# A two-layer deformable convolution in f32: the dense interpolation matmuls of layer 2 cut from 64x128 of the array and 384 columns to 64x64 and 352 columns

## What is computed

```python
x = x + L0(gn(x))    # 4 sampled positions a pixel, softmax weights, 1x1 projection, batch norm, gelu
x = x + L1(gn(x))    # 3x3 deformable convolution
```

```python
p = offset + p_0 + p_n                       # tap position, fractional
x_off = g_lt*gather(lt) + g_rb*gather(rb) + g_lb*gather(lb) + g_rt*gather(rt)
x_off = x_off * m                            # the gate
out = conv2d(x_off, w_conv, stride=3)        # sum over taps and channels
```

## Time and profile before

| | |
|---|---|
| median of three runs | 597.45 us |
| the profiled execution, its own time | 598.6 us |
| its span | 596.8 us |
| PE busy | 492.7 us (83%) |
| DVE busy | 453.8 us (76%) |
| GpSimd (POOL) busy | 379.1 us (64%) |
| ACT busy | 233.7 us (39%) |
| L1408, DVE multiply by the row hats | 144 instructions, some 950 ns each |
| L1416, DVE addition of row halves | 64 instructions, 955 ns |
| L993, PE dense interpolation | 640 records for 320 matmuls |

### The profile page before, as it was taken

The page is one execution under the profiler, slowest core; times in us unless marked ns, Lnnn a source line. Parts: engine busy times, 40 slices in busy tenths (PEclk is TensorE's granted clock), DMA queues, the critical chain, the costliest instruction groups (busy, mean ns, idle before and its releaser), DMA issues.

```text
span 596.8 us, 10350 instructions
## 1 busy us (share of the span) xinstructions
PE 492.7 (83%) x3568; PEld 296.3 (50%) x3568; DVE 453.8 (76%) x935; ACT 233.7 (39%) x407; POOL 379.1 (64%) x350
## 2 busy tenths in 40 slices
PE   0393699987740655989999999999999999999996
PEld 0271477665420422445555565555655555555554
DVE  2926489999648755576978878988898898898781
ACT  0543113321249557653434344334433433433311
POOL 5048167778725473564777777777777777777740
PEclk9975579999895756889999999999999999999999
DMA  9651746857400491121222222921221122122110
GB/s 196 170 182 36 167 101 142 175 125 165 107 24 0 150 115 28 35 58 32 74 78 72 72 71 72 120 54 49 56 56 53 51 54 58 49 54 55 52 39 11
DMA packets 44114, 48.58 MB, mean 81 GB/s; under 512 B 24858, under 2 KB 34458, under 8 KB 43556
## 3 DMA queue, kind: packets, MB, share of 16 engines
q1 hardware_dynamic: 33172, 25.67, 19.3%
q0 software_dynamic: 10752, 22.04, 14.6%
q10 hardware_dynamic: 144, 0.24, 0.2%
HBM read 39.01 MB, written 8.91 MB: 80 GB/s over the span
## 4 chain that ended last, share of the span: by engine, by line
PE 65%; DVE 10%; issue 7%; ACT 7%; POOL 5%; DMA 4%; SPq 1%; DVEq 0%; POOLq 0%; ACTq 0%
PE ps_later L993 9%; PE ps_pair L993 9%; PE ps_raw L977 8%; PE ps_x L1005 7%; PE ps_raw L836 6%; PE ps_o L1035 5%; PE ps_x L1014 4%; PE ps_x L1008 3%; PE ps_pair L816 3%; PE ps_o L849 3%; POOL got L496 3%; ACT xn L570 2%; PE ps_later L873 2%; PE ps_x L895 2%; DVE vlast L1408 2%
## 5 line engine op out<-in xcount | busy, mean ns | idle before, releaser
L496 POOL DMA_INDIRECT got<-table,idx x336 | 355.5, 1058 | 179.4 <-issue 123.0
L1408 DVE TENSOR_TENSOR vprod<-ps_pair,rhat 128x768 f32<-128x768 f32 x64 | 60.9, 952 | 7.5 <-PE ps_pair L993 7.4
L1599 DVE TENSOR_TENSOR prod<-got,wgt 128x512 f32<-128x512 f32 x84 | 57.4, 683 | 9.5 <-DMA got<-table,idx 9.3
L1408 DVE TENSOR_TENSOR vprod<-ps_later,rhat 128x768 f32<-128x768 f32 x64 | 60.6, 947 | 3.3 <-PE ps_later L993 3.2
L1416 DVE TENSOR_TENSOR vprod<-vprod 128x768 f32<-128x768 f32 x64 | 61.1, 955 | 1.2
L977 PE MATMUL ps_raw<-conv_out,later 128*128 128x512 f32 x96 | 58.7, 696 | 2.2 <-ACT shared L717 1.4
L1005 PEld LDWEIGHTS ps_x<-early,vprod 128*128 128x128 f32 x384 | 43.3, 144 | 33.0 <-issue 23.5
L1005 PE MATMUL ps_x<-early,vprod 128*128 128x128 f32 x384 | 55.1, 280 | 0.7 <-DVE vlast L1419 0.5
L1591 DVE TENSOR_TENSOR samples<-shared,vprod 128x800 f32<-128x800 f32 x44 | 42.9, 983 | 10.9 <-DMA shared<-positions 7.7
L816 PE MATMUL ps_pair<-early,xn 128*128 128x128 f32 (+1 forms) x136 | 21.0, 313 | 34.5 <-POOL xn L487 24.1
L704 ACT ACTIVATE samples<-ps_x 128x384 f32<-128x384 f32 x64 | 27.9, 488 | 53.9 <-PE ps_x L1014 53.5
(11 more groups left out here) (171 smaller groups left out, 813.5 us busy)
## 6 DMA issues: line engine op xcount, KB each, us to landing
shared<-positions SPq DMA_DIRECT2D x22, 440.0 KB, 6.3
table<-trow SPq DMA_DIRECT2D x24, 256.0 KB, 2.1
got<-table,idx POOLq DMA_INDIRECT x336
raw<-in_x SPq DMA_DIRECT2D x16, 256.0 KB, 10.0
y<-table SPq DMA_DIRECT2D x4, 512.0 KB, 8.2
out<-ysumT SPq DMA_DIRECT2D x64, 16.0 KB
later<-in_later SPq DMA_DIRECT2D x1, 514.5 KB
positions<-prow SPq DMA_DIRECT2D x2, 256.0 KB, 2.3
```

Of the source, the lines that this page charges most:

```text
L496: pool.indirect_dma_start(into[t][:, s * P:(s + 1) * P], None, tab, bass.IndirectOffsetOnAxis(ap=idx[:, slot, k:k + 1], axis=0),).then_inc ...
L1408: nc.vector.tensor_tensor(dst, ps_dense[pair_number(0, t, pair) % 2][:].rearrange("p (d n) -> p d n", d=2)[:, :, 0:WROWS * C].rearrange("p ...
L1599: nc.vector.tensor_tensor(into[:, t % 2, 0:S * P].rearrange("p (n c) -> p n c", c=C), came[:, t, 0:S * P].rearrange("p (n c) -> p n c", c= ...
```

## The change

A tile's two image rows get eleven rows of `xcol` each, instead of twelve together. A pair is four matmuls: for each image row `r` of the tile and each tap `h`, the weights are 64 x 64 of `chat` (the 64 pixels of that image row), the moving operand is 11 x 32 = 352 columns of `xcol` that begin one row lower for `r` = 1, and the result goes to partitions 64 `r` to 64 `r` + 63 of the tap's bank. `v_mm` counts four per pair. The row hats are built for 11 steps, and the table `grid1` loses the shift of one row for the second half of the partitions. DVE multiplies 2 x 11 x 32 = 704 elements. Of eleven rows, rows 6 to 10 are added to rows 0 to 4 and row 5 stays as it is, so PE still turns six rows.

```diff
-WROWS = 2 * REACH1 + 2
-XROWS = H - 1 + WROWS
+WROWS = 2 * REACH1 + 1
+XROWS = H + WROWS
+HALF = (WROWS + 1) // 2
...
-                    pe.wait_ge(v_mm, 2 * PAIRS * (g - 1))
+                    pe.wait_ge(v_mm, 4 * PAIRS * (g - 1))
...
-                for h in range(2):
-                    at, tap = (t + h, 8) if pair == 2 else (t, GT + 2 * pair + h)
-                    top = (g % GB) * GROWS + 2 * at + tap // 3 - 1
-                    nc.tensor.matmul(ps_dense[n % 2][:, h * GPIX:h * GPIX + WROWS * C],
-                                     chat[g % 2][W * h:W * (h + 1), pair, at * P:(at + 1) * P],
-                                     xcol[b][W * h:W * (h + 1), top * C:(top + WROWS) * C],
-                                     start=True, stop=True).then_inc(v_mm, 1)
+                for r in range(2):
+                    for h in range(2):
+                        at, tap = (t + h, 8) if pair == 2 else (t, GT + 2 * pair + h)
+                        top = (g % GB) * GROWS + 2 * at + tap // 3 - 1 + r
+                        nc.tensor.matmul(ps_dense[n % 2][W * r:W * (r + 1), h * GPIX:h * GPIX + WROWS * C],
+                                         chat[g % 2][W * h:W * (h + 1), pair, at * P + W * r:at * P + W * (r + 1)],
+                                         xcol[b][W * h:W * (h + 1), top * C:(top + WROWS) * C],
+                                         start=True, stop=True).then_inc(v_mm, 1)
...
-                for r in range(WROWS // 2):
+                for r in range(HALF):
...
-                    dve.wait_ge(v_mm, 2 * n + 2)
+                    dve.wait_ge(v_mm, 4 * n + 4)
...
-                half = WROWS // 2
+                half = WROWS - HALF
                 nc.vector.tensor_tensor(vprod[:, t % 2, 0:half, :], vprod[:, t % 2, 0:half, :],
-                                        vprod[:, t % 2, half:WROWS, :], ALU.add).then_inc(v_added, 1)
+                                        vprod[:, t % 2, HALF:WROWS, :], ALU.add).then_inc(v_added, 1)
...
-    grid1[:, GT:9] = REACH1 + (p // W)[:, None]
+    grid1[:, GT:9] = REACH1
```

More of the change, by code:

```diff
@@ L1003, in turn_samples @@
                     pe.wait_ge(trans_copied, n)
-                for r in range(WROWS // 2):
+                for r in range(HALF):
                     nc.tensor.matmul(ps_x[1][:, P:2 * P], vprod[:, t % 2, r, :], idn[:], start=(r == 0),
-                                     stop=(r == WROWS // 2 - 1), is_transpose=True)
-                for r in range(0, WROWS // 2, 2):
+                                     stop=(r == HALF - 1), is_transpose=True)
+                for r in range(0, HALF, 2):
                     last = nc.tensor.matmul(ps_x[1][0:2 * C, 2 * P:3 * P],
                                             vlast[:, t % 2, r:r + 2, :].rearrange("p w c -> p (w c)"), idn[:],
-                                            start=(r == 0), stop=(r + 2 == WROWS // 2), is_transpose=True)
+                                            start=(r == 0), stop=(r + 2 == HALF), is_transpose=True)
                 last.then_inc(v_turned, 1)
@@ L1414, in weigh_rows @@
                 dve.wait_ge(v_read, pairs_done(g, t))
-                half = WROWS // 2
+                half = WROWS - HALF
                 nc.vector.tensor_tensor(vprod[:, t % 2, 0:half, :], vprod[:, t % 2, 0:half, :],
-                                        vprod[:, t % 2, half:WROWS, :], ALU.add).then_inc(v_added, 1)
+                                        vprod[:, t % 2, HALF:WROWS, :], ALU.add).then_inc(v_added, 1)
                 if t % 2 == 0:
                     nc.vector.tensor_tensor(vlast[:, :, 0:half, :], vlast[:, :, 0:half, :],
-                                            vlast[:, :, half:WROWS, :], ALU.add).then_inc(v_added, 1)
+                                            vlast[:, :, HALF:WROWS, :], ALU.add).then_inc(v_added, 1)
             def next_gather_places(i, k, made):
```

## The result

| | before | after |
|---|---|---|
| median | 598.1 us (597.41 to 600.13, four runs) | 589.31 us (588.95 to 589.44) |
| profiled execution, its span | 598.6, 596.8 us | 589.18, 587.4 us |
| PE busy | 492.7 us | 480.7 us |
| DVE busy | 453.8 us | 431.5 us |
| one group, from group 7 on | 21.34 us | 20.42 us |

The ratio is 0.985 (95% 0.981 to 0.988), 8.8 us less. The forecast was 584.0, in a range of 581 to 590. One further execution of the changed kernel took 1141.93 us and is left out as disturbed.

The account below looks back on a forecast made before the run. PE was taken to bound the kernel, with DVE setting the pace for 0.23 us a group. PE's 12.6 and the waits' 1.0 gave 13.6 us off 598.6; the median forecast was 584.0 us, range 581 to 590.

Parts of the forecast that it names:

- rival 2: GpSimd sets the end: DVE's work adds 0.04 us to each of the last 144 gathers, 588 us; chance 0.15.
- What a pair is made of: PE's pair alone, 0.84 us before: 0.107 exposed weight load, 0.64 for two passes, about 0.095 wait before another shape.
- four matmuls of 64 x 64: PE's new pair: the four run together, load 0.053; 0.098 us less for a pair alone, 0.146 for a run of two.
- Rival 1: On PE, the four matmuls go two by two: a pair costs 1.38 us instead of 0.84, 678 us; chance 0.10.
- PE's part: Shorter pairs on PE in layer 2's groups, summed over groups 0 to 15: 12.6 us gained.
- DVE's waits: Two places in a group where PE waits for DVE; their shrinking gains 1.0 us, ends 0 and 1.6.
- DVE's operations: DVE's shorter L1408, L1416 and L1419: 885, 822 and 484 ns, worth nothing by themselves beside PE.
- The waits: PE's two waits for DVE, 0.23 us a group from group 7 on: 0.15 of it counted as gained.
- The two more counts: `v_mm` raised four times a pair, not two: 0 to 0.07 us on DVE's start, left at nothing, covered by DVE-PE balance.
- 7.5 - 5.5 leaves 2 us: GpSimd's lead at the last gather, 7.5 us, shrinks by 5.5 but still covers the faster loop; nothing is lost.
- The loop's 13.6: Layer 2's loop comes 13.6 us earlier at the end, from 12.6 for PE and 1.0 for the waits.
- GpSimd's 8.1: GpSimd's last gather comes 8.1 us earlier: 4.3 + 1.8 of removed waits and about 2 from groups 0 to 2.

Follow-up runs that it names:

- after_slots: The kernel after with eight slots instead of four for layer 2's gathers, everything computed: 586.2 us, ratio 0.978 to the kernel before.
- tiles_only: The kernel before with four 64 x 64 matmuls a pair, still on 384 columns: 765.15 us, ratio 1.023 to the kernel before on that chip.
- slots_one: The kernel after with eight gather slots and one count on `v_mm` a pair instead of four: 847.92 us, ratio 1.143 to the kernel before.
- columns_only: The kernel after with two 64 x 128 matmuls a pair on 352 columns: 748.55 us, beside 746.63 for the kernel before.
- short_adds_2: The kernel after with DVE's additions L1418 and L1421 cut to one row, repeated on a second chip: 783.05 us, beside 750.52.
- one_count: The kernel after with `v_mm` raised once a pair, on the last matmul, instead of four times: 770.27 us in one run, beside 746.63.
- short_adds: The kernel after with DVE's additions L1418 and L1421 cut to one row: 770.98 us, beside 746.63 for the kernel before.

## Why the prediction was right, and where it was off

- **The number.** Measured 589.3. The forecast of 584.0 missed by 5, and so did its own range of 581 to 587; the stated range holds 589.3 only because rival 2 had been given 586 to 590. That a miss of 5 us stayed inside is in part luck.
- **What a pair is made of; four matmuls of 64 x 64.** Forecast 0.749 alone and 1.49 - 0.146 = 1.344 for two; measured 0.75 and 1.34. That the four run together, with the load exposed in proportion to the weight columns, was read off L836, and holds. Rival 1 is out: the rule that loads overlap only when the row group differs (the Trainium skill, TensorE: Matmul & The Clock Gate, section "The mechanism") doesn't describe the row of four at 415.03, where two of them share their array rows.
- **PE's part and DVE's waits.** From the first weighing of group 2 to that of group 15 the kernel before takes 280.4 us (290.6 to 571.0) and `after_slots`, where DVE waits for no gather, 268.5 (290.4 to 559.0): 11.9 less. Forecast for these groups: 3.5 + 7.5 + 1.0 = 12.0. What follows to the last weighing is 0.7 shorter, forecast 0.6. The 1.0 for groups 0 and 1 is lost in the scatter of 4 us.
- **DVE's operations.** Forecast 885, 822 and 484 ns; measured 886, 823 and 486.
- **The waits.** Forecast to fall from 0.23 to 0.08 us a group, measured 0.12; the groups came to 20.42, forecast 20.4. The two more counts, left at nothing, cost 0.07, the upper end of the forecast's 0 to 0.07. On DVE's way of 3.10 us that makes 3.17 against PE's 3.15, and 0.02 is just what the transposes at 418.20 wait: the cover held but for that.
- **The step that failed: GpSimd, "7.5 - 5.5 leaves 2 us: nothing is lost, but it is close".** The loop's 13.6 was near enough. GpSimd's 8.1 was mis-sized. Counted from group 2, where both executions stand within 0.4 us (290.6 and 290.2), its last gather came 0.5 us earlier (283.8 against 283.3), not 6.1 (8.1 without the 2 for groups 0 to 2). Up to its group 7 it gained 3.3 (92.3 against 89.0) where 4.3 of removed waits were forecast: the loop got faster by 4 x 0.82 there, less than the waits held, so they were only shortened. From there to the last gather it lost 2.8 (191.5 against 194.2) where 1.8 more of gain was forecast. That is the larger error: the 21.1 us that GpSimd was said to need was read from a stretch in which GpSimd didn't run at its own pace but locked to DVE's; one turn of the loop shorter, it locked to 15 gathers a turn, and 16 take 21.67. The lead of 7.5 therefore fell short: 7.5 - 12.6 (the loop, 11.9 + 0.7) + 0.5 = -4.6 us, and the last weighing came 5.2 us later than in `after_slots` (286.5 against 281.2 us from group 2). The work that follows made up part of it, and 3 us were lost.
- **Rival 2** had the outcome: 588, with a chance of 0.15; measured 589.3. It had the mechanism in outline (gathers that stretch beside DVE's work), at 0.04 us a gather where 1.69 - 1.36 = 0.33 us a group is 0.02. The rest was the pace misread, so that its 588 lies so near the measured time is partly luck.
- **Why the shorter additions didn't help**, the point held against rival 2: what counts is not how long DVE's additions are in all (1.36 us of stretch a group before, 1.69 after), but at which of them a gather starts, and the lock decides that.

## What to carry over

An engine with slack doesn't have its own pace in the trace: before giving it a faster partner, find its bare cost (here 16 x 1.249 = 19.98 us a group) and what stretches each instruction, and ask whether the stretch shrinks too. Account for a lead over the whole run, not over a window; a lead of 7.5 us is spent by 1.25 us a group in six groups, and four more buffers bought 3 us back on the one chip where they ran. Where weights of half the columns suffice, splitting an f32 matmul into tiles that run together saves half the exposed part of its load (0.05 us here), at the price of more instructions and of 0.07 us for two more counts, which shows only where the next engine waits.

## What the runs showed of the hardware, unexpected

- Four f32 matmuls on 64 x 64 of the array, two of them on the same 64 rows, start in one row of the timeline and cost together what one does: 0.293 us a pass of 352 columns, and 0.053 for the load.
- An indirect DMA on GpSimd is held where a DVE instruction of over 0.3 us with two SBUF operands is running about 0.1 us after its start. It is held to that instruction's end, up to 0.62 us on 0.944. Two engines coupled in this way lock to a whole number of gathers a turn (16 in 21.34 us, 15 in 20.42). The lock was read from the traces; no run moved the additions or the gathers to break it.
- DVE starts 0.067 us behind the end of a pair that raises its semaphore once, 0.074 with two counts, and 0.145 with four.
- The same kernel took 598 us on one chip and 747, 751 and 759 on three others. Of the kernel before there is no trace from those; in the traces of the other kernels there, PE stands still, mostly for 0.3 to 1.7 us at a time, with nothing to wait for that the profile shows. The kernels with 4208 PE matmul records instead of 3568 were all slower there than the kernel before, `tiles_only` by 2.3% and `slots_one` by 14%; `columns_only`, with 3568, was level with it. The number of records is not all of it: `slots_one` took 8% more than `short_adds_2`, with 4208 too, on the same chip.
- The kernel after itself was not run there. Its nearest relatives were slower than the kernel before: `one_count` by 3.2% in one run, and `short_adds`, which leaves out most of two additions, by 3.3%, 4.3% and 5.1% in one run on each chip. So on such a chip the change most likely costs time where it gains 1.5% on the first. The cause is open.
